# The combine product of a soft mixture of experts: one true fp32 product, or three products of fp32r parts

## The reference

```python
x = x + xattn(layernorm(x), ctx, ctx, mask, ...)
y = layernorm(layernorm(x)) # norm_g, norm_b in the inner module
logits   = einsum('bnd,esd->bnes', y, layernorm(slot_embeds) * scale)
dispatch = softmax(logits, axis=1)                    # over the tokens
combine  = softmax(logits.reshape(b, n, E*S), axis=-1) # over all slots
slots = einsum('bnd,bnes->besd', y, dispatch)
gate  = gelu(einsum('besd,edf->besf', slots, Wg) + bg)
up    = einsum('besd,edf->besf', slots, Wu) + bu
eout  = einsum('besf,efo->beso', gate * up, Wd) + bd
x = x + einsum('bns,bso->bno', combine, eout)
```

## Time and profile before

| what | value |
|---|---|
| median of three runs | 1110.19 us (1107.48 to 1111.7) |
| span of the profiled execution | 1104.5 us |
| granted clock of TensorE, mean | 0.979 of full |
| PE, DVE, ACT, POOL busy | 1005.7, 805.8, 602.5, 429.7 us |
| combine products in the profile | 256 records, 65.6 us |

### The profile page before, as it was taken

The page is one execution under the profiler, slowest core; times in us unless marked ns, Lnnn a source line. Parts: engine busy times, 40 slices in busy tenths (PEclk is TensorE's granted clock), DMA queues, the critical chain, the costliest instruction groups (busy, mean ns, idle before and its releaser), DMA issues.

```text
span 1104.5 us, 22433 instructions
## 1 busy us (share of the span) xinstructions
PE 1005.7 (91%) x7440; PEld 671.8 (61%) x7440; DVE 805.8 (73%) x1427; ACT 602.5 (55%) x1084; POOL 429.7 (39%) x493
## 2 busy tenths in 40 slices
PE   5688899999986788878999999999999999999996
PEld 3466777777753444545666666656666666666664
DVE  5546677777766788857778788787787787877754
ACT  2367687787853888864353444443544534444421
POOL 5258776767765434328313132042131230420000
PEclk8889999999998999999999999999999999999999
DMA  7957786877741544454335235153343352452122
GB/s 213 192 122 141 158 155 161 155 161 144 159 106 50 171 113 100 124 129 150 77 93 149 49 79 169 30 154 93 80 129 92 82 161 39 106 141 45 29 68 80
DMA packets 122162, 128.38 MB, mean 116 GB/s; under 512 B 49556, under 2 KB 110472, under 8 KB 122072
## 3 DMA queue, kind: packets, MB, share of 16 engines
q1 hardware_dynamic: 108016, 85.51, 35.6%
q0 software_dynamic: 10896, 40.61, 12.3%
q10 hardware_dynamic: 3160, 1.11, 0.6%
HBM read 80.22 MB, written 29.96 MB: 100 GB/s over the span
## 4 chain that ended last, share of the span: by engine, by line
PE 52%; DVE 1%; issue 1%; ACT 1%; DVEq 0%; ACTq 0%
PE down L1883 15%; PE second L1324 15%; PE up L1324 7%; PE gate L1324 7%; PE mix L1829 5%; PE mix L1822 3%; DVE hid_l L1718 0%; DVE x L1689 0%; PE mix L1819 0%; ACT hid_h L1800 0%; DVE gate_sb L1706 0%; ACT wgu_h L1382 0%; DVE wd_l L1726 0%; ACT gate_sb L1783 0%; ACT slot_h L1769 0%
## 5 line engine op out<-in xcount | busy, mean ns | idle before, releaser
L426 POOL TENSOR_TENSOR p_l<-p_f,p_h 121x800 f16<-121x800 f32 (+1 forms) x96 | 163.5, 1718 | 78.8 <-ACT p_h L712 77.9
L535 DVE TENSOR_REDUCE head_max<-at_rows 100x2 f32<-100x722 f32 x124 | 112.9, 910 | 68.9 <-PE at_rows L790 67.1
L1800 ACT ACTIVATE hid_h<-gate_sb,hid_scale 128x512 f16<-128x512 f32 x128 | 91.9, 718 | 99.7 <-DVE gate_sb L1706 99.6
L1883 PE MATMUL down<-wd_h,hid_h 128*128 128x256 f16 x512 | 140.2, 274 | 5.2 <-DVE hid_l L1718 4.9
L1883 PE MATMUL down<-wd_h,hid_l 128*128 128x256 f16 x512 | 140.4, 274 | 0.0
L1883 PE MATMUL down<-wd_l,hid_h 128*128 128x256 f16 x512 | 140.2, 274 | 0.0
L1783 ACT ACTIVATE gate_sb<-gate,bgu,un_gate 128x512 f32<-128x512 f32 x63 | 48.8, 775 | 150.9 <-PE gate L1324 150.9
L1718 DVE SCALAR_TENSOR_TENSOR hid_l<-gate_sb,hid_scale,hid_h 128x512 f16<-128x512 f32 x128 | 101.0, 789 | 19.7 <-ACT hid_h L1800 16.4
L707 ACT ACTIVATE p_f<-at_cols 121x800 f32<-121x800 f32 (+1 forms) x96 | 79.6, 829 | 25.9 <-PE at_cols L812 24.7
L1370 POOL DMA_DIRECT2D bd<-in_bd x16 | 9.0, 563 | 212.4 <-DVE eo L1740 212.4
L712 ACT ACTIVATE p_h<-p_f 121x800 f16<-121x800 f32 (+1 forms) x96 | 83.6, 871 | 3.0
(11 more groups left out here) (218 smaller groups left out, 2525.1 us busy)
## 6 DMA issues: line engine op xcount, KB each, us to landing
eo_pair<-eo SPq DMA_DIRECT2D x128, 128.0 KB, 2.6
k_parts<-kq_n SPq DMA_DIRECT2D x16, 724.0 KB, 3.6
kt<-k_parts SPq DMA_DIRECT2D x32, 362.0 KB
wgu<-in_Wg POOLq DMA_DIRECT2D x16, 512.0 KB, 5.4
wgu<-in_Wu POOLq DMA_DIRECT2D x16, 512.0 KB, 6.8
wd<-in_Wd POOLq DMA_DIRECT2D x16, 512.0 KB, 5.3
combine<-combT SPq DMA_DIRECT2D x16, 400.0 KB, 4.4
dispatch<-dispT SPq DMA_DIRECT2D x16, 400.0 KB
```

The source lines that it names most:

```text
L426: nc.gpsimd.tensor_tensor(p_l[i][0:kn, :, 0:N], p_f[i][0:kn], p_h[i][0:kn, :, 0:N], ALU.subtract).then_inc(p_low, 1)
L535: nc.vector.tensor_reduce(head_max[:, :, r], bank[0:N, :, 0:S], AX.X, ALU.max).then_inc(max_ready, 1)
L1800: nc.scalar.activation(hid_h[:, c, :], gate[c % 2][:], ACT.Copy, scale=keep["hid_scale"][:, bass.ds(ex, 1)]).then_inc(hidh_ready, 1)
L1883: mm = nc.tensor.matmul(down_ps[t // 2][:, t % 2, :], ht[:, c, t * P:(t + 1) * P], wt[:, c, :], start=(c == 0 and k == 0), stop=(c == FC - ...
```

## The change

The combine's two operands are held as two fp32r parts each: `comb_h`, `comb_l` and `eo_h`, `eo_l`. The DMAs bring the fp32 values into the tiles of the low parts; ACT copies them to the high part (rounded to fp32r), POOL subtracts the high part in place. Each fp32 product becomes three fp32r products summed in PSUM (high x high, low x high, high x low). The last half step (`LAST` = 15) skips the split and multiplies the fp32 values as before. The combine weights are loaded by halves of the batches, with a semaphore each. Eight semaphores of the attention stage are cleared on POOL at the start of the routing stage, and six of them are used again for the new waits. POOL's order of loads and splits is rewritten around the new work.

```diff
+    keep["spent"] = [st_done, p_f_ready, p_hi, p_low, pv_done, k_done, v_done, q_done]
...
     def _(pool):
+        for spent in keep["spent"]:
+            pool.sem_clear(spent)
...
-    comb = sb("comb", [P, B, N], F32)
+    comb_l, comb_h = sb("comb_l", [P, B, N], F32R), sb("comb_h", [P, B, N], F32R)
...
-    eo_pair = [sb(f"eo_pair{i}", [P, BH, D], F32) for i in range(2)]
+    eo_l = [sb(f"eo_l{i}", [P, BH, D], F32R) for i in range(2)]
+    eo_h = [sb(f"eo_h{i}", [P, BH, D], F32R) for i in range(2)]
+    LAST = 2 * (E // 2) - 1
...
-                    dst = eo_pair[h][e * SL:(e + 1) * SL].rearrange("s (t two) d -> s t two d", two=2)
+                    dst = eo_l[h][e * SL:(e + 1) * SL].bitcast(F32).rearrange("s (t two) d -> s t two d", two=2)
...
-        pool.dma_start(comb[:], combine_dram[0]).then_inc(comb_in, 16)
+        for h in range(2):
+            hb = slice(BH * h, BH * h + BH)
+            pool.dma_start(comb_l[:, hb].bitcast(F32), combine_dram[0][:, hb]).then_inc(comb_in[h], 16)
...
+        def load_combine_weights(pair, h):
+            pool.wait_ge(comb_done, 4 * (2 * pair + h - 1))
+            ... (DMA of one half)
+        def combine_weights_lo(hs, h):
+            pool.wait_ge(combh_ready, hs + 1)
+            for q in range(2):
+                bs = slice(BH * h + 4 * q, BH * h + 4 * q + 4)
+                nc.gpsimd.tensor_tensor(comb_l[:, bs], comb_l[:, bs].bitcast(F32), comb_h[:, bs].bitcast(F32), ALU.subtract)...
+        def outputs_lo(hs, h, r):
+            pool.wait_ge(eoh_ready, 4 * hs + r + 1)
+            bs = slice(2 * r, 2 * r + 2)
+            nc.gpsimd.tensor_tensor(eo_l[h][:, bs], eo_l[h][:, bs].bitcast(F32), eo_h[h][:, bs].bitcast(F32), ALU.subtract)...
...
         def step(pair, first, last):        # POOL, the new order
+            if not last:  load_weights(pair, 0)
+            if not first:
+                for r in range(4): outputs_lo(hs - 1, 1, r)
+                load_combine_weights(pair, 0)
+            if not last:
+                load_slot_weights(pair + 1, 0, hs + 2)
+                split_tokens(0, BH) if first, else split_slot_weights(pair + 1, 0, hs + 2)
+                load_weights(pair, 1)
+                load_down_weights(pair, 0)
+                (first: split_tokens(BH, B), split_slot_weights)
+            combine_weights_lo(hs, 0)
+            if not last:  load_down_weights(pair, 1)
+            if not first: load_combine_weights(pair, 1)
+            if not last:  load_slot_weights(pair + 1, 1, hs + 3)
+            for r in range(4): outputs_lo(hs, 0, r)
+            if not last:
+                split_slot_weights(pair + 1, 1, hs + 3)
+                combine_weights_lo(hs + 1, 1)
+                (loads of the down biases, as before)
...
+        def outputs_hi(hs, h, r):           # ACT
+            for x in range(2):
+                act.wait_ge(eo_moved[h][x][r // 2], 32 * (hs // 2) + 32)
+            bs = slice(2 * r, 2 * r + 2)
+            nc.scalar.activation(eo_h[h][:, bs], eo_l[h][:, bs].bitcast(F32), ACT.Copy).then_inc(eoh_ready, 1)
+        def combine_weights_hi(pair, h):
+            act.wait_ge(comb_in[h], 16 * pair + 16)
+            nc.scalar.activation(comb_h[:, hb], comb_l[:, hb].bitcast(F32), ACT.Copy).then_inc(combh_ready, 1)
...
                             (gelu of chunk c)
+                        if prev and e == 0:
+                            outputs_hi(hs - 1, 1 - h, c)
+                        if e == 1 and c == 1 and nxt:
+                            combine_weights_hi(pair, h)
                         if h == 0 and c == 0:
                             (wd_h)
...
-                mm = nc.tensor.matmul(mix_ps[1 - r % 2][0:N, i * D:(i + 1) * D], comb[:, BH * h + j, :], eo_pair[h][:, j, :], start=True, stop=True)
+                if hs == LAST:
+                    mm = nc.tensor.matmul(dst, cl.bitcast(F32), el.bitcast(F32), start=True, stop=True)
+                else:
+                    for k, (ct, et) in enumerate(((ch, eh), (cl, eh), (ch, el))):
+                        mm = nc.tensor.matmul(dst, ct, et, start=(k == 0), stop=(k == 2))
...
-                            if r % 2 == 0:
-                                for x in range(2):
-                                    pe.wait_ge(eo_moved[1 - h][x][r // 2], 32 * pair + 32 * h)
+                            pe.wait_ge(eol_ready, 4 * (hs - 1) + r + 1)
                             if r == 0:
-                                pe.wait_ge(comb_in, 16 * pair + 16 * h)
+                                pe.wait_ge(combl_ready, 2 * hs)
...
+                    if r == 0:
+                        pe.wait_ge(comb_in[1], 16 * pair + 16)
```

More of the change, by code:

```diff
@@ L1551, in expert_phase, with cleared @@
     eo = [sb(f"eo{e}", [P, ROWS // P, D], F32) for e in range(2)]
-    eo_pair = [sb(f"eo_pair{i}", [P, BH, D], F32) for i in range(2)]
-    comb_in = sem("comb_in")
+    eo_l = [sb(f"eo_l{i}", [P, BH, D], F32R) for i in range(2)]
+    eo_h = [sb(f"eo_h{i}", [P, BH, D], F32R) for i in range(2)]
+    LAST = 2 * (E // 2) - 1
+    def cleared(name):
+        return ctx.enter_context(nc.semaphore(name, num=keep["spent"].pop().num))
+    comb_in = [cleared(f"comb_in{h}") for h in range(2)]
+    combh_ready, combl_ready = cleared("combh_ready"), cleared("combl_ready")
+    eoh_ready, eol_ready = cleared("eoh_ready"), cleared("eol_ready")
     slot_parts = sem("slot_parts")
@@ L1634, in split_slot_weights @@
                 split(disp_h[:, bs], disp_l[:, bs], disp[:, bs], 2 * B + BH * (hs - 2) + 2 * q)
+        def load_combine_weights(pair, h):
+            pool.wait_ge(comb_done, 4 * (2 * pair + h - 1))
+            pool.sem_inc(waited, 1)
+            hb = slice(BH * h, BH * h + BH)
+            pool.dma_start(comb_l[:, hb].bitcast(F32), at(combine_dram, pair)[:, hb]).then_inc(comb_in[h], 16)
+        def combine_weights_lo(hs, h):
+            pool.wait_ge(combh_ready, hs + 1)
+            pool.sem_inc(waited, 1)
+            for q in range(2):
+                bs = slice(BH * h + 4 * q, BH * h + 4 * q + 4)
+                nc.gpsimd.tensor_tensor(comb_l[:, bs], comb_l[:, bs].bitcast(F32), comb_h[:, bs].bitcast(F32), ALU.subtract).then_inc(combl_ready, 1)
@@ new lines, in outputs_lo, with load_weights @@
+        def outputs_lo(hs, h, r):
+            pool.wait_ge(eoh_ready, 4 * hs + r + 1)
+            pool.sem_inc(waited, 1)
+            bs = slice(2 * r, 2 * r + 2)
+            nc.gpsimd.tensor_tensor(eo_l[h][:, bs], eo_l[h][:, bs].bitcast(F32), eo_h[h][:, bs].bitcast(F32), ALU.subtract).then_inc(eol_ready, 1)
+        def load_weights(pair, e):
+            pool.wait_ge(wl_ready[e], pair + 1)
+            if pair > 0:
+                pool.wait_ge(eo_moved[1][e][1], 32 * pair)
+            pool.sem_inc(waited, 1)
+            load_gate_up(pool, a, keep, e, pair + 1)
@@ L1636, in step, with load_down_weights @@
+        def load_down_weights(pair, e):
+            pool.wait_ge(wdl_ready[e], pair + 1)
+            pool.sem_inc(waited, 1)
+            load_down(pool, a, keep, e, pair + 1)
         def step(pair, first, last):
+            hs = 2 * pair
             if not last:
-                for e in range(2):
-                    pool.wait_ge(wl_ready[e], pair + 1)
-                    if not first:
-                        pool.wait_ge(eo_moved[1][e][1], 32 * pair)
-                    pool.sem_inc(waited, 1)
-                    load_gate_up(pool, a, keep, e, pair + 1)
-                    if e == 0:
-                        load_slot_weights(pair + 1, 0, 2 * pair + 2)
-                        if first:
-                            split_tokens(0, BH)
-                        else:
-                            split_slot_weights(pair + 1, 0, 2 * pair + 2)
@@ L1650, in step @@
-                pool.wait_ge(wdl_ready[0], pair + 1)
-                pool.sem_inc(waited, 1)
-                load_down(pool, a, keep, 0, pair + 1)
+                load_weights(pair, 0)
+            if not first:
+                for r in range(4):
+                    outputs_lo(hs - 1, 1, r)
+                load_combine_weights(pair, 0)
+            if not last:
+                load_slot_weights(pair + 1, 0, hs + 2)
+                if first:
+                    split_tokens(0, BH)
+                else:
+                    split_slot_weights(pair + 1, 0, hs + 2)
+                load_weights(pair, 1)
+                load_down_weights(pair, 0)
@@ L1661, in step @@
-                pool.sem_inc(waited, 1)
-                pool.dma_start(comb[:], at(combine_dram, pair)).then_inc(comb_in, 16)
+                load_combine_weights(pair, 1)
             if not last:
-                load_slot_weights(pair + 1, 1, 2 * pair + 3)
-                split_slot_weights(pair + 1, 1, 2 * pair + 3)
+                load_slot_weights(pair + 1, 1, hs + 3)
+            for r in range(4):
+                outputs_lo(hs, 0, r)
+            if not last:
+                split_slot_weights(pair + 1, 1, hs + 3)
```

(2 more changed lines are left out.)

13 lines of the change are left out of this document (8 added, 5 removed).

## The result

The changed kernel takes 1104.3 us (median of 20 runs, 1101.51 to 1110.53) against 1109.25 us (20 runs, 1104.09 to 1115.89): the ratio of the runs on record is 0.9963, 95% interval 0.995 to 0.9977. That ratio makes 4.1 us of the prediction's 1110.19, where the forecast had 4.0; the two medians lie 4.95 apart, which the interval covers too.

The account below looks back on a forecast made before the run. The experts' stage was taken to last as long as PE's instruction stream. Terms -5.4 (rounds behind chunk 1) + 1.4 (ACT) - 1.3 + 1.3 (shared interface) = -4.0 us took 1110.19 to 1106.2, range 1100.5 to 1113.

Parts of the forecast that it names:

- The round behind chunk 3 is worth nothing: Before the down product: PE would stand 0.25 us for `hid_l`, whose chain omits the combine; 30 rounds x 0.
- The round behind chunk 1 pays in full: Ahead of chunk 2's gate and up, whose waits are long met: 30 x 0.18 = 5.4 us saved (3.0 to 6.3).
- ACT before `wd_h`: h=0, e=0 of pairs 1 to 7: `outputs_hi` delays `wd_h` by 0.9, costing PE 7 x 0.2 = 1.4 us.
- The shared interface: equal: POOL's work stretching DVE's `hid_l`: 1.3 us of old contention goes and 7 x 0.18 = 1.3 comes, taken as equal.
- The outputs land late: Rival, 0.12: ACT waits for the outputs' move before `wd_h`; past 2.4 us each 0.1 costs PE 0.1 in seven places.
- The clears cost nothing: Eight semaphore clears on POOL at the routing stage's start: between 0 and 1.6 us, taken as 0.
- an fp32r round is no cheaper: Rival, 0.11: at 0.143 us a product the combine round stays 0.86, giving 1111.6 us, no change.
- both rounds pay: Rival, 0.17: the chain up to `hid_l` has slack, so 60 x 0.18 - 1.4 = 9.4 us saved, 1100.8.

Follow-up runs that it names:

- e1: Changed kernel with the rounds behind chunk 3 back to one true fp32 product of the high parts: 1105.61 us, 0.9975 of the kernel before.
- e2: Changed kernel with the rounds behind chunk 1 back to one true fp32 product of the high parts: 1108.15 us, 1.0 of the kernel before.
- e3: Changed kernel with DVE's `hid_l` of chunk 3 in two halves of 256 columns: 1100.03 us, 0.9917 of the kernel before.
- e11: e9 with POOL's combine and slot weight loads of h=1 started behind the first `outputs_lo`: 1095.01 us, 0.9871 of the kernel before.
- e9: e3 with the down weights' split in h=0 moved to chunk 1 for e=0 alone: 1099.5 us, 0.9911 of the kernel before.
- e4: Kernel before the change with `hid_l` of chunk 3 in two halves, true fp32 kept: 1104.02 us, 0.9965 of the kernel before.
- e8: e4 with the down weights' split in h=0 moved from chunk 0 to chunk 1: 1105.89 us, 0.9969 of the kernel before.
- e6: Changed kernel without splitting copies and subtractions, its three fp32r products reading unsplit tiles: 1104.05 us, 0.9967 of the kernel before.
- e12: e9 run once more, unchanged, beside e11: 1097.65 us, 0.989 of the kernel before.
- e10: e3 run once more, unchanged, on the same chip as e9: 1099.84 us, 0.9915 of the kernel before.

## Why the prediction was right, point by point

The time came out as forecast (0.9963 x 1110.19 = 1106.1 against 1106.2), and the two main steps held. That it came out within 0.1 us is luck: some terms were off and made up for each other, and one late output and one early first round, neither in the sum, all but cancel in the profile. By the profiled executions, with the forecast in brackets:

- *The round behind chunk 3 is worth nothing.* Held. 30 x 0.154 = 4.6 us are spared and 30 x 0.14 = 4.2 are stood (0.06 to 0.20, forecast 0.06 to 0.25). 0.4 is left (0). e1 and e2 show it one way, e3 the other.
- *The round behind chunk 1 pays in full.* Held in kind. 30 x 0.154 = 4.6 us (5.4). The step that was off is the product's price: 0.118 from start to start, not 0.113, between the bounds of 0.109 and 0.126. By the rule of the Trainium skill ("FP8 and Floating Point Precision", TensorE Precision Notes: four passes for true FP32), with one pass for each fp32r product as the prediction took it, the round would have saved 0.215; the products are a little dearer than a quarter of a true one.
- *ACT before `wd_h`.* 0.05 to 0.08 lost in seven places, 0.4 us (1.4). `wd_h` was late as forecast; of the 0.2 a place, 0.09 goes since the copy takes 0.63 and not 0.72, and 0.03 since the round is shorter by 0.154 and not by 0.18.
- *The shared interface: equal.* Held by the sums, not by the places. What is stood beyond the usual is 3.4 - 30 x 0.06 = 1.6 us before and 7.6 - 30 x 0.20 = 1.6 after. In each, 0.36 is one unit of h = 1 (pair 3, e = 1) that stands alike in both. Five places in h = 0, e = 0 made the other 1.3 before and are gone. (The prediction had them from the earlier trace rows, as 2.3 us in five waits beside "the tail's 2.6". That reading is wrong: the 2.6 and a 1.2 belong to the very first unit, at 503.7 and 499.7 us, which has no combine round, and only two of the six waits are in h = 0, e = 0 behind a round. The size is right all the same, since most of these places stand too little to be listed.) The prediction looked at `outputs_lo` and the splits of h = 1, and none of those shows in the standing; what hits `hid_l` is the subtraction in `comb_l` in e = 1, 1.3 us in two places. These two, both h = 0, in the timeline of the changed kernel, with a third that costs PE nothing:

```profile
673.41 2.03 POOL L1662 TENSOR_TENSOR comb_l<-comb_l,comb_h 128x400 fp32r<-128x400 f32 x2
674.62 1.39 DVE L1766 SCALAR_TENSOR_TENSOR hid_l<-gate_sb,hid_scale,hid_h 128x512 f16<-128x512 f32 x1 [0.25 <-ACT hid_h L1868]
...
748.64 2.50 POOL L1662 TENSOR_TENSOR comb_l<-comb_l,comb_h 128x400 fp32r<-128x400 f32 x2
749.18 1.05 DVE L1766 SCALAR_TENSOR_TENSOR hid_l<-gate_sb,hid_scale,hid_h 128x512 f16<-128x512 f32 x1 [0.25 <-ACT hid_h L1868]
...
898.04 2.04 POOL L1662 TENSOR_TENSOR comb_l<-comb_l,comb_h 128x400 fp32r<-128x400 f32 x2
898.38 2.25 DVE L1766 SCALAR_TENSOR_TENSOR hid_l<-gate_sb,hid_scale,hid_h 128x512 f16<-128x512 f32 x1 [0.25 <-ACT hid_h L1868]
```

  `hid_l` of chunk 1 takes 1.39 and 2.25 in place of 0.75, the chain of chunks 2 and 3 is behind by that much, and PE stands 0.42 and 1.25 in the down product. The rows also say what sets the length: `hid_l` ends 0.57 and 0.55 behind the end of POOL's second subtraction (675.44 and 900.08), whether it had begun 0.8 or 1.7 before that end, so it seems to stand still while POOL works. In the third place the first of the two subtractions ends at 749.68, `hid_l` 0.55 later, and the second subtraction takes 1.50 in place of 1.03: there DVE came in between the two, and POOL was the one held up.
- *The outputs land late* (the rival on the slower side, 0.12). It happened once, in h = 1 and not at the forecast's place: 1.8 us. The reason given against it, that the weight loads go out behind the moves, is true of the gate and up weights in h = 0; in h = 1 the loads of combine and slot weights go out in front. In e11 they don't, but e9 has no such wait with the old order, so the order by itself is not the whole cause.
- *The clears cost nothing.* Held. From the last score product of the attention to the first product of the logits it is 29.3 us in both profiles; in the fourteen it is 29.3 to 29.7 without the clears (three) and 29.2 to 30.6 with them, so a cost of some tenths could hide there.
- *Not in the sum:* the first combine round of all starts 1.5 us sooner behind the logits. In the kernel before PE's list of waits, 520 to 1080 us, has one of 1.2 us there, with no releaser, and it is absent after. It doesn't come of loading `comb` in one piece: e4, which does so too, has no such wait, and from the last product of the logits its first round starts after 57.3 us, sooner than in any profile with the halves (57.6 to 60.6), while e8 needs 61.8. So it is a spread between executions and no work of the change.

These terms are -0.4 - 4.6 + 0.4 + 0 + 1.8 - 1.5 = -4.3 us, and -3.5 were read between the logits and the end; of the 0.8 between them about 0.3 are chunks ahead of the slots, a hundredth longer each, and the rest isn't assigned. The rival that an fp32r round is no cheaper falls by the 3.455 and 3.30. The rival that both rounds pay falls for this kernel by the standing (4.2 us stood again, and gone in e1), and comes true once `hid_l` is halved: by the standing in e3, and by the time from the first round to the last down product in e9 and e11.

## What to carry to other kernels

When an engine that bounds a stage gets shorter work, ask at each place whether its next semaphore moves too: here half of the 9.2 us spared on PE was stood again in front of a chain of three engines that had no slack, and halving the last link of that chain brought about as much again as the new products had (0.46% and 0.37%). A copy or subtraction that runs in another engine's idle time may cost nothing (e6), but loads that are still under way when a small move on the critical path starts can make that move late (e12, e10), so look at when they land and not only at when they are started; starting them behind the move avoids it (e11). Try such an edit on the old kernel as well (e4, e8): some 0.35% of the gain of e3 had nothing to do with fp32r.

## What the runs showed of the hardware

- Products of 256 columns of fp32r with 100 weight columns start every 0.118 us, against 0.109 for fp16 with 128, and 0.108 for each fourth of a true fp32 product of 0.43. The first of a run is listed about 0.19 early, while its weights load (0.306 to the next start instead of 0.118).
- Two inputs of 128x512 in SBUF on DVE (`hid_l`) take 0.75 us alone and 0.93 to 2.25 beside POOL's two-input work. The Trainium skill ("GPSIMD Engine Reference", Specifications) says that the two share their SBUF interfaces; that the price may be threefold is what the trace adds. In the rows above `hid_l` ends 0.55 to 0.57 behind the end of a subtraction, so its length goes by what was left of POOL's work when it began: 1.39 with the second subtraction left, 2.25 with both. Why DVE waited for both at 898.38 and came in between at 749.18 stays open.
- A subtraction of 128x512 into fp32r on POOL takes 1.27 us undisturbed, 1.35 in the mean.
- A move of 128 KB from SBUF to SBUF lands in 2.4 us. With two loads from DRAM started some 4 us ahead of it, it took 2.9 where these landed 1.5 and 2.5 us after its start (e9, pair 1), and up to 5.9 where both were still on their way 2.8 us after it (e10, pairs 1 and 4).
